# A two-layer sequence model: routing of the head mixture spread over its neighbours, and the scan's skip term on TensorE

## The reference

```python
# head mixture: routing
logits = normalize(x) @ normalize(sim) - sigmoid(gates)     # 16 experts
gated  = relu(logits)             # a token with no positive logit keeps its two largest
rw     = softmax(where(mask > 0, gated, -inf))
q, k, v = sum_e rw[e] * (x @ proj[e])                        # proj[e]: 256 x 64 each
# ... one causal attention with q, k, v, then sum_e (attn * rw[e]) @ o_proj[e]

# selective scan, for 512 channels d and 16 states n
h[d,n] = exp(dt[d]*A[n]) * h[d,n] + dt[d]*u[d]*B[n]
y[d]   = sum_n h[d,n]*C[n] + u[d]*D[d]                       # u*D is the skip term
out    = (y * silu(z)) @ W_out
```

## Time and profile before

| | us |
|---|---|
| median of 3 runs | 4489.09 (4488.7 to 4492.88) |
| the profiled execution | 4494.44 |
| its span, from first to last instruction | 4492.6 |
| of it in the loop of layer 0 | about 4 x 457 |

### The profile page before, as it was taken

The page is one execution under the profiler, slowest core; times in us unless marked ns, Lnnn a source line. Parts: engine busy times, 40 slices in busy tenths (PEclk is TensorE's granted clock), DMA queues, the critical chain, the costliest instruction groups (busy, mean ns, idle before and its releaser), DMA issues. The chain is left out here.

```text
span 4492.6 us, 39616 instructions
## 1 busy us (share of the span) xinstructions
PE 3576.0 (80%) x13112; PEld 2012.1 (45%) x13168; DVE 3243.8 (72%) x4803; ACT 1407.8 (31%) x2360; POOL 1796.4 (40%) x874
## 2 busy tenths in 40 slices
PE   5799879987988798777778677777777786777769
PEld 2577557765766486632223322224322233222234
DVE  4566456545754476469997679995699976799955
ACT  3222322232223222253332343331533323433310
POOL 1101210121003000309995049991099950499910
PEclk9899989998989899899999889998999998899989
DMA  3000100010001000206663136661066631366530
GB/s 126 1 19 1 57 1 10 10 57 1 1 20 58 1 1 19 90 11 217 209 206 131 34 123 211 210 202 61 10 218 209 207 131 35 122 209 209 204 107 7
DMA packets 156471, 421.74 MB, mean 94 GB/s; under 512 B 21713, under 2 KB 58961, under 8 KB 154465
## 3 DMA queue, kind: packets, MB, share of 16 engines
q1 hardware_dynamic: 156258, 419.03, 27.4%
HBM read 392.20 MB, written 26.78 MB: 93 GB/s over the span
## 5 line engine op out<-in xcount | busy, mean ns | idle before, releaser
L1376 POOL TENSOR_TENSOR hc<-h,c_sb 128x1024 f32<-128x1024 f32 x344 | 806.0, 2352 | 622.5 <-DMA c_sb<-bc_rows 550.7
L1304 PE MATMUL PS<-hc,ident 128*128 128x512 f32 x1376 | 712.4, 644 | 89.7 <-POOL hc L1376 75.0
L1345 ACT ACTIVATE da<-dt,a_neg 128x1024 f32<-128x1024 f32 x384 | 437.7, 1141 | 501.5 <-DVE h L1401 501.4
L1287 PE MATMUL PS<-bc,pick 128*128 128x512 bf16 x712 | 237.5, 414 | 300.6 <-DVE h L1401 265.8
L1384 DVE TENSOR_TENSOR PS<-dtu,PS 128x1024 f32<-128x1024 f32 x384 | 461.4, 1202 | 5.4 <-PE PS L1287 5.4
L1304 PEld LDWEIGHTS PS<-hc,ident 128*128 128x128 f32 x1376 | 257.7, 200 | 425.2 <-issue 207.8
L1401 DVE TENSOR_TENSOR_SCAN h<-da,state,PS 128x1024 f32<-128x1024 f32 x192 | 443.3, 2328 | 0.0
L1401 DVE TENSOR_TENSOR_SCAN h<-da,PS 128x1024 f32<-128x1024 f32 x192 | 431.3, 2268 | 0.0
L100 POOL TENSOR_TENSOR ln_rstd<-ln_var,eps_pow 128x4 f32<-128x4 f32 x65 | 71.4, 1105 | 849.8 <-DVE ln_var L93 849.8
L689 DVE SCALAR_TENSOR_TENSOR acc<-PS,rw,acc 128x192 f32<-128x192 f32 x768 | 285.0, 413 | 174.5 <-ACT acc L721 91.1
L1376 POOL TENSOR_TENSOR tok<-h,c_sb 128x1024 f32<-128x1024 f32 x168 | 395.1, 2352 | 33.7 <-DVE h L1401 24.5
(11 more groups left out here) (251 smaller groups left out, 6552.1 us busy)
## 6 DMA issues: line engine op xcount, KB each, us to landing
c_sb<-bc_rows SPq DMA_DIRECT2D x512, 512.0 KB, 4.2
bu<-bc_rows SPq DMA_DIRECT2D x64, 512.0 KB, 5.4
tok<-bc_rows SPq DMA_DIRECT2D x64, 512.0 KB, 5.5
xT<-in_xT SPq DMA_DIRECT2D x5, 2048.0 KB, 7.5
tok<-in_x SPq DMA_DIRECT2D x4, 2048.0 KB, 9.6
x_after_layer<-tok SPq DMA_DIRECT2D x16, 512.0 KB, 3.0
xT_after_layer<-x2T_out SPq DMA_DIRECT2D x16, 512.0 KB, 2.8
x2T<-xT_after_layer SPq DMA_DIRECT2D x16, 512.0 KB, 3.7
```

Source lines behind the costliest of these rows:

```text
L1287: op = pe.matmul(bank(at + j), pick[:, row, :], bc3[:, half * HALF + j * CHUNK:half * HALF + (j + 1) * CHUNK], start=True, stop=True)
L1304: op = pe.matmul(bank(Y + j), ident[:, :], hc_at[v % 3][:, j * CHUNK:(j + 1) * CHUNK], start=(n == 0), stop=(n == N - 1))
L1345: act.activation(decay_at(v), dt[:, m, at], ACT.Exp, scale=a_neg[:, n:n + 1]).then_inc(dr, 1)
L1376: pool.tensor_tensor(hc_at[v % 3], h[:, v % 3, :], c_sb[:, v % 3, :], ALU.mult).then_inc(hr, 1)
```

## The change

Two independent changes.

**Routing.** The block of its own is gone. The squares, the root and the matmuls with `simn` go into the block at the end of the wave branch, group by group: on ScalarE four squares ahead of each group's two copies, on TensorE `logits(g)` (four tiles) among the last transposes, on GpSimd a root for each group. The matmuls now have 16 columns, and all logits fit one bank, number 5, which is why the products with `wout` go through five banks. VectorE's chain (`gating`) opens its queue in the block of the head projections. ScalarE's first `weigh` waits for it (semaphore `gd`), and TensorE's slab 5 of tile 0, in bank 5, waits until the logits have been read (`lt`).

**Scan.** `skip` holds diag(D) for each of the four groups of channels, made once. `through_skip(r)` multiplies u by it on TensorE and opens the sum of the round in banks 0 and 1, so that the 16 gathers add to it. `collect_y` is now a copy on ScalarE, placed after step 0 of the next round. The wait for it (`yd`) moves from the gather of step 0 to `through_skip`. The saved states lie in `kept` instead of a tile of their own.

```diff
@@ wave_branch, second block
+    first.close()                      # dep_late, feat_tmp and qf give their memory to sq
+    sq = tile(s, "sq", [P, 2, D])
...
+            def logits(g):
+                pe.wait_ge(ln1.copied, 2 * g + 2)
+                for i in range(4 * g, 4 * g + 4):
+                    for k in range(KC):
+                        last = pe.matmul(bank(5)[:, i * EXPERTS:(i + 1) * EXPERTS], xT[:, k, i * P:(i + 1) * P],
+                                         simn[:, k, 0:EXPERTS], start=(k == 0), stop=(k == KC - 1))
+                last.then_inc(lr, 1)
...
-                if i >= 6:
-                    pe.wait_ge(su, i - 5)
+                if i >= 5:
+                    pe.wait_ge(su, i - 4)
...
                 if i in (10, 14):
                     ln1.transpose(pe, (i - 10) // 4)
+            logits(0)
             ln1.transpose(pe, 2)
+            logits(1)
             ln1.transpose(pe, 3)
+            logits(2)
+            logits(3)
...
             for g in range(TILES // 4):
+                act.wait_ge(ln1.done, g + 1)
+                for i in range(4 * g, 4 * g + 4):
+                    if i >= 2:
+                        act.wait_ge(sr, i - 1)
+                    act.activation(sq[:, i % 2, :], tok[:, i, :], ACT.Square, accum_out=ss[:, i:i + 1])\
+                       .then_inc(sr, 1)
                 ln1.copy(act, g)
...
+            def norm(g):
+                w = slice(4 * g, 4 * g + 4)
+                pool.wait_ge(sr, 4 * g + 4)
+                pool.tensor_tensor(rs[:, w], ss[:, w], half_pow[:, w], ALU.pow).then_inc(sp_, 1)
             for g in range(TILES // 4):
                 ln1.root(pool, g)
+                if g >= 2:
+                    norm(g - 2)
+            norm(TILES // 4 - 2)
+            norm(TILES // 4 - 1)
@@ head_mixture: the routing block goes, its VectorE part opens the next block
+                        if i == 0 and j == 5:
+                            pe.wait_ge(lt, 1)
...
+                def gating():
+                    dve.wait_ge(sp_, TILES // 4)
...
+                    dve.wait_ge(lr, TILES // 4)
+                    dve.tensor_tensor(lg[:, :, :], bank(5)[:, 0:TILES * EXPERTS].rearrange(...),
+                                      wide(rs[:, :]), ALU.mult).then_inc(lt, 1)
...
+                    dve.tensor_tensor(rw[:, :, :], ex[:, :, :], wide(ss[:, :]), ALU.mult).then_inc(gd, 1)
+                gating()
                 for i in range(TILES):
...
                 def weigh(i):
+                    if i == 0:
+                        act.wait_ge(gd, 1)
...
                 round_x(0)
                 round_x(1)
+                act.wait_ge(le, 1)
+                act.activation(ex[:, :, :], lg[:, :, :], ACT.Exp).then_inc(lx, 1)
@@ layer1 setup
+                    for m in range(KI):
+                        dve.tensor_scalar(skip[:, m, :], ident[:, :], dskip[:, m:m + 1], None, ALU.mult)
@@ scan
-        state = tile(g, "state", [P, KI, STATE])
+        state = kept[:, 0, 0:KI * STATE].rearrange("p (m n) -> p m n", n=STATE)
...
+                def through_skip(r):
+                    m, _, at = where(r)
+                    if r:
+                        pe.wait_ge(yd, r)
+                    for j in range(2):
+                        pe.matmul(bank(Y + j), skip[:, m, :], u[:, m, at.start + j * CHUNK:at.start + (j + 1) * CHUNK],
+                                  start=True, stop=False)
+
                 def gather(v):
                     r, n = units[v]
+                    if n == 0:
+                        through_skip(r)
                     pe.wait_ge(hr, v + 1)
-                    if n == 0 and r:
-                        pe.wait_ge(yd, r)
...
+                def collect_y(r):                       # on ScalarE; was scalar_tensor_tensor on VectorE
+                    m, _, at = where(r)
+                    act.wait_ge(yr, N * (r + 1))
+                    act.activation(dt[:, m, at], bank(Y, 2), ACT.Copy).then_inc(yd, 1)
...
+                for v, (r, n) in enumerate(units):
                     save(v)
                     if v + 2 <= last:
                         decay(v + 2)
+                    if n == 0 and r:
+                        collect_y(r - 1)
+                collect_y(len(rounds) - 1)
```

More of the change, by code:

```diff
@@ L345, in layer0 @@
         tok = tile(L, "tok", [P, TILES, D])
+        ss, rs = tile(L, "ss", [P, TILES]), tile(L, "rs", [P, TILES])
         with nc.Fori(0, BATCH) as b:
@@ L357, in wave_branch @@
 def wave_branch(nc, t, b, s, tile, sem, bank, ident, tok, xT, wqkvg, bq, bg_half, bout, wout, toep, cct,
[L358 removed]
+                layer_norm, simn, half_pow, ss, rs):
     qg = tile(s, "qg", [P, KC, SEQ])
     dep = tile(s, "dep", [P, KC, FIELD])
[L362 to L364 removed]
     tail = tile(s, "tail", [P, KC, CHUNKS])
@@ L368, in wave_branch @@
     lastg = tile(s, "lastg", [P, KC])
+    first = s.enter_context(ExitStack())
+    dep_late = tile(first, "dep_late", [P, 2, CHUNK])
+    tmp = tile(first, "feat_tmp", [P, 2, 5, CHUNK])
+    qf = tile(first, "qf", [P, 2, CHUNK])
     proj, feat, used = sem("proj_ready"), sem("feat_ready"), sem("proj_used")
@@ L614, in head_mixture @@
-    with ExitStack() as g:
+        sp_, lr, lt, le, lx = (sem(n) for n in ("norm_root", "logits_mm", "logits_taken", "logits", "logits_exp"))
+        gd = sem("weights_done")
         acc = tile(g, "acc", [P, 2, 4, QKV])
@@ L977, in layer1 @@
             a_neg = tile(W, "a_neg", [P, STATE])
+            skip = tile(W, "skip", [P, KI, P])
             pick = tile(W, "pick", [P, STATE, P], BF16)
@@ L1024, in layer1 @@
                 with ExitStack() as s:
-                    state_space(nc, b, s, tile, sem, bank, ident, tok, xT, w_in, w_dt, w_x, w_out, cw, cb, bdt, dskip,
+                    state_space(nc, b, s, tile, sem, bank, ident, tok, xT, w_in, w_dt, w_x, w_out, cw, cb, bdt, skip,
                                 a_neg, pick, bc3, x2_dram, x2T_dram, bc_dram, kept, layer_norm, out)
@@ L1029, in layer1, with state_space @@
             experts(nc, t, out, s, tile, sem, bank, ident, ones, kept, layer_norm)
-def state_space(nc, b, s, tile, sem, bank, ident, tok, xT, w_in, w_dt, w_x, w_out, cw, cb, bdt, dskip, a_neg, pick, bc3,
+def state_space(nc, b, s, tile, sem, bank, ident, tok, xT, w_in, w_dt, w_x, w_out, cw, cb, bdt, skip, a_neg, pick, bc3,
                 x2_dram, x2T_dram, bc_dram, kept, layer_norm, out):
@@ L1413, in _ @@
                         times_u(v + 1)
-                    if n == 2 and r:
-                        collect_y(r - 1)
                     scan(v)
-                collect_y(len(rounds) - 1)
     with ExitStack() as g:
```

119 lines of the change are left out of this document (42 added, 77 removed).

## The result

| | before | changed |
|---|---|---|
| median | 4488.9 us (4484.25 to 4492.88) | 4425.64 us (4422.22 to 4430.39) |
| ratio, 95% interval | | 0.986 (0.9843 to 0.9877) |
| the profiled execution | 4494.44 us | 4430.39 us |

The change makes the kernel 63 us faster. The direction was as forecast, the size was not: 99.6 us were expected and 4425.64 lies outside the range of 4376 to 4418. Between the two profiled executions the time divides as follows. A part's border is ScalarE's first table load in it; "at 1.2 GHz" sums the stretches with a granted clock of 0.50.

What follows compares the result with a forecast made beforehand. No single engine bounds the kernel: the limit changes by stage, with TensorE and VectorE idle at the routing and VectorE pacing the scan. Routing 66.8 plus scan 32.8 gave 99.6 us off, so 4390 us, range 4376 to 4418.

Steps and rivals of the forecast that it cites:

- the price of a logits pass: Routing, TensorE: a pass of 16 columns costs 0.113 us, as with 128 columns; other end 0.22 to 0.26.
- the sum has 15.4: Routing: first slab pass at 621.0 instead of 636.37, 15.4 us gained for each sequence.
- Rival A: Routing: narrow logits passes are dear, 0.22 us each, so 10.3 us gained a sequence instead of 15.4; 4410 us; 20%.
- The clock gain: First slab passes after routing: less half-level clock as TensorE's idling shrinks, 1.3 us a sequence, between 0 and 2.85.
- 66.8 were forecast: Routing in all four sequences: 4 x (15.4 + 1.3) = 66.8 us gained.
- VectorE's chain hidden: Routing: VectorE's 9.0 us chain runs behind TensorE's tile 0 slabs; cost 0, other end 1 us for each sequence.
- The margin of 0.1 us: Routing: third weight there at 629.3, TensorE at tile 1 at 629.4 at the earliest; 3 us where TensorE starts slowly.
- rival B: Routing: the chain isn't hidden, the third weight comes late at tile 1; up to 3 us a sequence, 4400 us; 10%.
- 28 x 1.17: Scan: `collect_y` leaves VectorE at 28 round starts, 1.17 us each, 32.8 us gained.
- the allowance for TensorE's lateness: Scan, round boundary: TensorE late now and then at the half level, 1 us off in all, other end 12.
- rival D: Scan, round start: TensorE's chain at half level becomes the bound, 5.1 us late a round; slower, 4532 us; 2.5%.
- Rival C: Scan: keeps its pace, since GpSimd or the loads of its rows take over; 4422 us; 5%.

Runs made afterwards that it cites:

- the combined kernel: Changed kernel with logits passes of 128 columns, the skip product ahead of the spread of step 4, and GpSimd's memset of v last: 4393.0 us, ratio 0.9787.
- the other execution of the old layer 0: Kernel before with only layer 1 (the scan) taken from the changed kernel, layer 0 as it was: 4458.12 us, ratio 0.9936.
- the wide run: Changed kernel with logits passes padded to 128 columns, into banks 1 to 4, instead of 16 columns into bank 5: 4410.85 us, ratio 0.9829.
- the filler: The combined kernel plus four unread matmuls of 256 columns in TensorE's wait ahead of the third group of transposes: 4389.85 us, ratio 0.9785.
- with the gap filled: Changed kernel, 16-column logits kept, plus four unread matmuls of 256 columns in TensorE's wait ahead of the third group of transposes: 4405.33 us, ratio 0.9811.

## Why the prediction was wrong

**The step that failed: the price of a logits pass.** It took 0.113 us, "the cost lies in loading 128 columns of weights, and narrowing the moving side saves nothing". At full clock that holds: 0.115 with 16 columns (16 in 1.85), 0.12 with 128 (16 in 1.95). What it left out is that narrowing the moving side costs the clock. With 16 columns 48 of 64 records took 0.21 and the transposes between them 1.95 instead of 1.04. So the first slab came 13.9 us behind the last scale on average instead of 8.2, and 9.8 us were gained where the sum has 15.4: 4 x 5.6 = 22 us of the 36 that are missing. That it is the width, the same 64 records in the kernel before show (7.38 us with 128 columns, 11.40 with 16, both begun at full clock). Rival A had the number (0.22, 10.3 us a sequence) for another reason, a dear pass; its single row had been read as 1.2 GHz by its loads of 333 ns, and the loads at 1.2 GHz in the changed kernel bear that out (L460 in 603 to 615: 333). The step used that reading to set the row aside instead of asking why it should be otherwise in the new place.

**The clock gain** of 1.3 us a sequence was none: the first slabs still start at 1.2 GHz, 36 passes take 10.0 to 11.2 us (before: 10.0 to 11.3). On average they are 0.2 us longer than before, so with the 1.3 this is 6 us in four sequences. The forecast expected the gain from filling pauses. With wide passes it was there (9.0 us in the combined kernel, 10.7 before), so the sum's mechanism was right for another kernel: there the first slab comes 14.5 us earlier than before and the 36 passes are 1.65 us shorter, 4 x 16.2 = 65 us where 66.8 were forecast. Layer 0 as a whole says 66.7 (1902.6 to 1835.9), or 58.6 against the other execution of the old layer 0 (1894.5).

The forecast named the Trainium skill here, "TensorE: Matmul & The Clock Gate", section "What's actually happening": the low level is the default and sustained activity releases it. The wide passes of the combined kernel agree with that (0.50 in 597 to 599, 1.00 from 600, with TensorE busy). Narrow passes show that TensorE busy for 12.00 of 12.00 us can stay at 0.50, and the measurement decides.

**VectorE's chain hidden: right, by the slow slabs alone.** It took 10.1 us (615.62 to 625.70) instead of 9.0, as L648 took 0.94 instead of 0.17 and L656 0.71 instead of 0.43. The margin of 0.1 us that the prediction gave it at full clock would not have held. It stayed hidden since the slabs began at 1.2 GHz, the case for which the prediction had 3 us to spare. With fast slabs, in the wide run, it cost 1.01 us a sequence by the mechanism of rival B.

**The scan: 28 x 1.17 right, the allowance for TensorE's lateness too small.** The rounds gave 28 x 1.19 = 33.3 us. TensorE's lateness, put at 1 us with 12 as the other end, was 3 x 1.71 + 1.03 + 4 x 0.75 = 9.2. The working had gone through a round in the middle, at full clock. It missed the first round, in which the kernel before has no wait for y and so no 1.17 to give, while the changed one has a product more, behind a wait of 6.24 us. GpSimd and ScalarE did not become the bound, and something of rival D's mechanism (TensorE's chain at a round's start at 1.2 GHz) did occur, in 8 of 32 rounds and at 1.7 and 0.75 us instead of 5.1.

Forecast to result: 99.6 - 22.4 (passes) - 6.0 (clock) - 8.2 (lateness beyond the 1 us) + 0.5 (rounds) = 63.5, measured 63. That the three terms meet the total so closely is in part luck, since the same code differed by 5 to 8 us between executions. Rival C's 4422 lies nearest to the measured time by chance: the scan did not keep its pace.

What stays open: how passes of a width between 32 and 128 columns would run, and why the clock stayed up through a gap of 2.21 us in one sequence (the second of the wide run) and fell within 1.1 us behind the same gap in the other seven with wide passes. Whether the filler's gain is given back in layer 0 or was lost by chance was not told apart.

## What to carry to other kernels

Don't price a row of TensorE work by one figure: look at the granted clock of the stretch in which it will run, and at how many columns each pass feeds, since here padding the passes from 16 to 128 columns cost nothing at full clock (1.85 and 1.95 us for 16) and let the slabs behind them start at 2.4 instead of 1.2 GHz, their first 14 passes in 3.4 instead of 4.8 to 6.1 us. Put new TensorE work into a wait that is already there, ahead of what the critical engine waits for and not behind it, and work it out for the first round as well as for a middle one. When an edit makes a hidden chain's cover shorter, look for what runs beside that chain.

## What the runs showed of the hardware

- TensorE busy without a pause let its clock fall from 2.4 to 1.2 GHz when its passes had 16 columns against 128 columns of weights (at 620.7 in the kernel before with narrow passes; with transposes among them, at 605.4 with the gap filled). Where the passes began at 1.2 GHz, 64 of 16 columns ran at it to their end (13.81 us); with 32 columns it was the same as with 16 (0.213 us a record); with 128 columns the clock was back at 2.4 GHz 3.5 us after they began (164.7, first sequence before).
- At full clock 16, 32 and 128 moving columns cost the same: 16 fp32 records in 1.85, 1.87 and 1.95 us.
- A VectorE operation on 128x16 elements took 0.94 us beside a GpSimd memset that reads nothing, and 0.17 without it. The Trainium skill, "SBUF — State Buffer", section "SBUF: two separate sides", has the two engines share a pair of ports as an exclusive lock, the later one waiting out the other's whole instruction; the 0.94 agree, as the memset ran from 615.58 for 0.95 us and the operation, begun at 615.62, ended with it.
